# Input tokens stored as one contiguous piece per load, and the last output bank's last products done in two halves

## The reference

```python
hidden = relu(x @ wi.T + 2*(x @ common_wi_a.T) @ common_wi_b.T + 2*(x @ Ab.T) @ Bb.T)   # 256 -> 1024
h      = hidden @ wo.T + (the same two corrections)                                     # 1024 -> 256
probs  = softmax(h.mean(axis=1) @ gate_w);  top_w, top_i = top_k(probs, 2);  top_w /= top_w.sum()
y      = sum over the 2 chosen e of  top_w[e] * (gelu(h @ w1[e] + b1[e]) @ w2[e] + b2[e])
return x + y
```

## Time and profile before

| what | us |
|---|---|
| median of 3 runs (lowest, highest) | 267.82 (267.65, 268.33) |
| the profiled execution | 267.44 |
| its span in the trace, first to last event | 265.6 |
| what lies around the span | 1.8 |
| PE busy | 261.0 |
| DVE / ACT / POOL busy | 173.7 / 174.7 / 160.7 |

### The profile page before, as it was taken

The page is one execution under the profiler, slowest core; times in us unless marked ns, Lnnn a source line. Parts: engine busy times, 40 slices in busy tenths (PEclk is TensorE's granted clock), DMA queues, the critical chain, the costliest instruction groups (busy, mean ns, idle before and its releaser), DMA issues.

```text
span 265.6 us, 3607 instructions
## 1 busy us (share of the span) xinstructions
PE 261.0 (98%) x1150; PEld 212.7 (80%) x1150; DVE 173.7 (65%) x283; ACT 174.7 (66%) x279; POOL 160.7 (60%) x192
## 2 busy tenths in 40 slices
PE   8999999999999999999999999999999999999994
PEld 2778888888888888888888888888888888888883
DVE  0783767375999726667595866657856567565664
ACT  2757464555466379988986887676777677675650
POOL 2076998934389877798539999456366366331100
PEclk9999999999999999999999999999999999999999
DMA  5995120201042112201202112202202206000004
GB/s 185 346 389 202 42 79 0 84 1 39 0 123 79 12 67 82 79 16 64 83 0 50 65 46 79 79 0 82 69 13 79 79 2 199 0 0 2 0 1 158
DMA packets 11139, 19.76 MB, mean 74 GB/s; under 512 B 2000, under 2 KB 2256, under 8 KB 10992
## 3 DMA queue, kind: packets, MB, share of 16 engines
q1 hardware_dynamic: 10544, 18.61, 20.9%
q10 hardware_dynamic: 576, 0.92, 1.0%
HBM read 17.43 MB, written 2.10 MB: 74 GB/s over the span
## 4 chain that ended last, share of the span: by engine, by line
PE 98%; DVE 0%; DVEq 0%; issue 0%
PE out_ps L754 16%; PE out_ps L755 16%; PE out_ps L758 16%; PE hid_ps L754 14%; PE hid_ps L755 14%; PE hid_ps L758 14%; PE hid_ps L943 2%; PE hid_ps L794 1%; PE out_ps L872 1%; PE hid_ps L798 1%; PE hid_ps L802 1%; PE hid_ps L894 1%; PE hid_ps L884 1%; DVE x_sb L1242 0%; DVEq L130 0%; DVE y_sb L1143 0%
## 5 line engine op out<-in xcount | busy, mean ns | idle before, releaser
L409 POOL TENSOR_TENSOR up_lo<-up_raw,up_hi 128x512 fp32r<-128x512 f32 x41 | 52.9, 1312 | 37.5 <-ACT up_hi L569 37.4
L754 PE MATMUL out_ps<-hid_hi,down_hi 128*128 128x512 f32 x192 | 75.0, 390 | 0.0
L755 PE MATMUL out_ps<-hid_lo,down_hi 128*128 128x512 f32 x192 | 74.8, 390 | 0.0
L758 PE MATMUL out_ps<-hid_hi,down_lo 128*128 128x512 f32 x192 | 74.8, 390 | 0.0
L754 PE MATMUL hid_ps<-act_hi,up_hi 128*128 128x512 f32 x166 | 65.0, 392 | 0.0
L755 PE MATMUL hid_ps<-act_lo,up_hi 128*128 128x512 f32 x166 | 64.8, 390 | 0.0
L758 PE MATMUL hid_ps<-act_hi,up_lo 128*128 128x512 f32 x166 | 64.7, 390 | 0.0
L601 ACT ACTIVATE hid_ps<-hid_ps,bias_sb 128x512 f32<-128x512 f32 x64 | 42.2, 659 | 29.1 <-DVE hid_ps L1064 18.0
L1038 DVE SCALAR_TENSOR_TENSOR hid_lo<-hid_ps,mix,hid_hi 128x512 fp32r<-128x512 f32 x64 | 47.9, 748 | 20.2 <-ACT hid_hi L615 19.6
L415 POOL TENSOR_TENSOR down_lo<-down_raw,down_hi 128x512 fp32r<-128x512 f32 x24 | 32.3, 1348 | 37.2 <-ACT down_hi L579 37.2
L615 ACT ACTIVATE hid_hi<-hid_ps,mix 128x512 fp32r<-128x512 f32 x64 | 44.1, 689 | 4.7
(11 more groups left out here) (91 smaller groups left out, 237.0 us busy)
## 6 DMA issues: line engine op xcount, KB each, us to landing
up_raw<-in_w SPq DMA_DIRECT2D x16, 256.0 KB, 2.7
down_raw<-in_w SPq DMA_DIRECT2D x16, 256.0 KB, 2.5
lora_raw<-in_lora SPq DMA_DIRECT2D x10, 256.0 KB, 5.0
down_raw<-in_woT SPq DMA_DIRECT2D x8, 256.0 KB, 3.4
up_raw<-in_wiT SPq DMA_DIRECT2D x7, 256.0 KB, 4.3
outT<-x_sb SPq DMA_DIRECT2D x6, 256.0 KB, 3.6
x_sb<-in_xT SPq DMA_DIRECT2D x1, 1024.0 KB, 8.4
x_sb<-in_xT SPq DMA_DIRECT2D x1, 512.0 KB, 5.6
```

What stands on the lines that cost most here:

```text
L409: ins = eng.tensor_tensor(up_lo[:, n, cols], up_raw[:, n, cols], f32(up_hi[:, n, cols]), ALU.subtract)
L754: eng.matmul(out, w_h, a_h, start=start, stop=False, skip_group_check=onto)
L755: eng.matmul(out, w_h, a_l, start=False, stop=False, skip_group_check=onto)
L758: return eng.matmul(out, w_l, a_h, start=False, stop=stop, skip_group_check=onto)
```

## The change

The host stores `x` in three arrays instead of one: `x0T` [2 blocks, 128, 512] for the two loads of L262, `x0bT` [128, 2, 512] for the load of L327, and `x1T` for sequence 1. Each of the first three loads then reads one unbroken piece of DRAM. The load of sequence 1 was unbroken already. Number, order, size and queue of the DMAs stay.

At the end, the last output bank (1,1) is treated otherwise. Its sum in `out_ps[:, 3]` ends with set 22 (the `stop` mark moves there). A new function `last_half` makes the last set's products for this bank over 256 tokens at a time, the first half into bank 0 of `hid_ps` and the second into bank 1, whose hidden tiles have been read by then. Each half raises `s_done`. DVE first adds the bank of set 22, the bias and `x` over all 512 tokens (`with_bias`, semaphore `s_last`), right after its last `hid_low`, and later adds each half with a plain two-operand addition.

```diff
 def load_x0(eng, kd):
-    eng.dma_start(x_sb[:, 0, 0, kd, :], xT[0, :, 0, kd, :]).then_inc(s_x0[kd], 16)
+    eng.dma_start(x_sb[:, 0, 0, kd, :], x0T[kd, :, :]).then_inc(s_x0[kd], 16)
...
-            eng.dma_start(x_sb[:, 0, 1, :, :], xT[0, :, 1, :, :]).then_inc(s_x0b, 16)
+            eng.dma_start(x_sb[:, 0, 1, :, :], x0bT[:, :, :]).then_inc(s_x0b, 16)
...
+        LAST_BANK = {3: 0, 4: 1}
...
+                ends = q in GROUP_LAST or (q == NSET - 2 and (kd, t) == ENDS[-1])
                 return three(out_ps[:, bank, :], (down_hi[:, n, cols], down_lo[:, n, cols]),
                              (hid_hi[:, j, :], hid_lo[:, j, :]), q in GROUP_FIRST and j == mine[0],
-                             q in GROUP_LAST and j == mine[1], low_ready)
+                             ends and j == mine[1], low_ready)
+
+            def last_half(n):
+
+                q, (kd, _, toks) = NSET - 1, FINAL[n]
+                for j in (1, 3):
+                    f = tiles(q)[j][0]
+                    cols = slice(f * D + kd * P, f * D + (kd + 1) * P)
+                    ins = three(hid_ps[:, LAST_BANK[n], toks], (down_hi[:, q % ND, cols], down_lo[:, q % ND, cols]),
+                                (hid_hi[:, j, toks], hid_lo[:, j, toks]), j == 1, j == 3)
+                ins.then_inc(s_done, 1)
...
-                for kd in range(KD):
-                    for j in (1, 3):
-                        if kd == 0:
-                            eng.wait_ge(s_hid_lo, 4 * q + j + 1)
-                        ins = down_pair(q, j, kd)
-                    ins.then_inc(s_done, 1)
+                for j in (1, 3):
+                    eng.wait_ge(s_hid_lo, 4 * q + j + 1)
+                    ins = down_pair(q, j, 0)
+                ins.then_inc(s_done, 1)
+                for n in LAST_BANK:
+                    last_half(n)
...
+            def with_bias(kd, t, cols):
+                x = x_sb[:, NB - 1, t, kd, cols]
+                return eng.scalar_tensor_tensor(out=x, in0=out_ps[:, kd * NT + t, cols],
+                                                scalar=mixed_b2[:, NB - 1, 1, kd:kd + 1], in1=x,
+                                                op0=ALU.add, op1=ALU.add)
+
+
+            eng.wait_ge(s_down, 4 * (NSET - 1))
+            with_bias(*ENDS[-1], slice(0, TOK)).then_inc(s_last, 1)
             for n, (kd, t, cols) in enumerate(FINAL):
-                x = x_sb[:, NB - 1, t, kd, cols]
-                eng.wait_ge(s_done, ENDS.index((kd, t)) + 1)
-                eng.scalar_tensor_tensor(out=x, in0=out_ps[:, kd * NT + t, cols],
-                                         scalar=mixed_b2[:, NB - 1, 1, kd:kd + 1], in1=x,
-                                         op0=ALU.add, op1=ALU.add).then_inc(s_final, 1)
+                eng.wait_ge(s_done, n + 1)
+                if n not in LAST_BANK:
+                    with_bias(kd, t, cols).then_inc(s_final, 1)
+                else:
+                    x = x_sb[:, NB - 1, t, kd, cols]
+                    eng.wait_ge(s_last, 1)
+                    eng.tensor_tensor(x, hid_ps[:, LAST_BANK[n], cols], x, ALU.add).then_inc(s_final, 1)
...
+    by_partition = x.reshape(NB, S // TOK, TOK, D // P, P).transpose(0, 4, 1, 3, 2)
     arrays = {
         "ids": a["itok_B_0_7"].reshape(1, NB),
-        "xT": x.reshape(NB, S // TOK, TOK, D // P, P).transpose(0, 4, 1, 3, 2),
+        "x0T": by_partition[0, :, 0].swapaxes(0, 1),
+        "x0bT": by_partition[0, :, 1],
+        "x1T": by_partition[1],
```

More of the change, by code:

```diff
@@ L17, with build @@
 TOP_K = 2
-def build(nc, ids, xT, wiT, woT, early, lora, gate, w1, w2, b12, outT):
+def build(nc, ids, x0T, x0bT, x1T, wiT, woT, early, lora, gate, w1, w2, b12, outT):
     D, NTOK = outT.shape
@@ L198, in build @@
         s_x0hi, s_up0hi = sem("s_x0hi"), sem("s_up0hi")
-        s_r2, s_r3, s_add, s_hid_lo, s_merge, s_raw_lo, s_sum_lo, s_fin, s_final = (
-            sem(n) for n in ("s_r2", "s_r3", "s_add", "s_hid_lo", "s_merge", "s_raw_lo", "s_sum_lo", "s_fin", "s_final"))
+        s_r2, s_r3, s_add, s_hid_lo, s_merge, s_raw_lo, s_sum_lo, s_fin, s_final, s_last = (
+            sem(n) for n in ("s_r2", "s_r3", "s_add", "s_hid_lo", "s_merge", "s_raw_lo", "s_sum_lo", "s_fin", "s_final",
+                             "s_last"))
         s_up0lo, s_merge0, s_tok = sem("s_up0lo"), sem("s_merge0"), sem("s_tok")
@@ L336, in _ @@
             load_lora(0, 4, e)
-            eng.dma_start(x_sb[:, 1, :, :, :], xT[1, :, :, :, :])\
+            eng.dma_start(x_sb[:, 1, :, :, :], x1T[:, :, :, :])\
                .then_inc(s_x1, 16)
```

## The result

The changed kernel takes 266.70 us (median of 21, 265.86 to 267.52); the kernel before, timed beside it, 268.33 (median of 21, 266.85 to 271.15). The ratio is 0.9941, 95% interval 0.9923 to 0.9958: 1.6 us less, where 0.4 was forecast.

What follows compares the result with a forecast made beforehand. The prediction took PE's work plus the stretches before its first and behind its last instruction as the bound. Its terms, loads 0, DVE -0.36, extra addition 0, last store -0.05, gave -0.4 from 267.82: 267.4 us, range 266.9 to 268.2.

Steps and rivals of the forecast that it cites:

- The end: Last output bank, its additions and last store: DVE -0.36 us and store -0.05 us, together about -0.4 us.
- Pace of the halves: PE's last bank: twelve matmuls of 256 columns start 0.12 us apart, so PE ends 0.08 us later.
- DVE's last result: Behind PE's end only one addition of 0.44 us remains, so the last store can be issued 0.36 us earlier.
- The additions of 512: DVE's extra addition over 512 tokens fits into its gaps and does not move the third addition: 0 us.
- The last store: With the DMA engines nearly to itself it lands slightly sooner: 0 to -0.2 us, taken as -0.05.
- (a): Rival, last bank: halved matmuls pay the full weight load; chance 0.06 at 268.2 us or beyond, 0.05 at 267.7.
- (b): Rival, end: stores bunch and the last one's landing grows by what it was issued earlier; no gain, 267.8 us, chance 0.12.
- surplus of 390 ns: Last bank: by the skill's issue gaps, twelve halves would cost PE 390 ns more than six wholes, instead of 80.
- The loads of x: 0 us: Start of the kernel: faster loads of x gain nothing; bounds -0.3 and +0.1 us.
- the dummy matmuls hide all three: Start: dummy matmuls and PE's first products cover all three changed loads of x, so their landing does not matter.
- slack of 0.8 us: Third load of x: PE takes its operand 0.8 us after it is ready, so a load that much slower costs nothing.
- Rival (c): An earlier third load of x removes PE's pause at 18.45 us: another 0.3 us less, 267.1 us, chance 0.12.

Runs made afterwards that it cites:

- e2: The changed kernel with the loads of x as before, so only the last output bank in halves: 267.96 us, ratio 0.9997 to the kernel before.
- e1: The kernel before with only the loads of x made unbroken, its end unchanged: 266.86 us, ratio 0.9944.
- e14: The kernel before, unchanged, profiled again; one of its long executions: 270.93 us.
- e13: The kernel before with the load of lora_first moved behind the two strided loads of x on SP's queue: 273.86 us, ratio 1.0187.
- e7: The kernel before with lora_first, always of expert 0, loaded as ACT's first DMA, loads of x strided: 267.18 us, ratio 0.9955.
- e12: The kernel before, unchanged, profiled again: 268.16 us.
- e6: The kernel before with only the third load of x (512 KB, second token half) made unbroken: 268.89 us, ratio 1.0009.
- e3: The whole changed kernel timed once more, on the same chip as its parts: 266.54 us, ratio 0.9926 to the kernel before.
- e5: The kernel before with only the two 256 KB block loads of x made unbroken: 267.44 us, ratio 0.9953.
- e10: The kernel before with only the load of x of block 1 (SP's second DMA) made unbroken: 267.45 us, ratio 0.9975.
- e11: The changed kernel with 9 dummy matmuls instead of 12: 266.22 us, ratio 0.9914 to the kernel before.
- e16: The changed kernel with 10 dummy matmuls instead of 12: 266.46 us, ratio 0.9918 to the kernel before.
- e9: The kernel before with only the load of x of block 0 (ACT's first DMA) made unbroken: 267.49 us, ratio 0.9969.
- e8: The changed kernel with 24 dummy matmuls instead of 12: 269.03 us, ratio 1.0025 to the kernel before.

## Why the prediction was wrong

**The end: right, by its steps.** Pace of the halves 0.12: 0.119. DVE's last result 0.36 earlier against PE's first product of the last bank: 0.39, since the addition took 0.42 and not 0.44. The additions of 512 didn't move the third one: it starts 0.20 us behind the last bank's first matmul in both profiles. The last store: -0.05 was taken, 0 was seen. The sum of 0.4 was 0.4 in the profiles; the timings of e2 alone can't tell it from zero. Rivals (a) and (b) fell, and with the first the rule of the Trainium skill that was weighed there ("TensorE: Matmul & The Clock Gate", "Back-to-back issue gap"): in place of its surplus of 390 ns stand 12 x 0.119 - 6 x 0.226 us, 70 ns.

**The loads: the step that failed.** "The loads of x: 0 us" was -1.2 (1.6 less the end) to -1.5 (the ratio of e1). The bound for it was -0.3. The lower end of the range rests on that bound; the words behind it (267.1 less 0.3) give 266.8 and not the 266.9 that is written, and 266.7 lies below both. Three things in that step were wrong.

First, it asked who waits for x and not what else is delayed by moving x. The load of `lora_first` stands between those of x, and PE's first real product needs it. Its name was in the list of DMAs, its landing (2.65 + 2.8 = 5.5) against the dummies' end (6.4) was never set down as a cover of 0.9 us that could shrink. With the unbroken block loads `lora_first` took 2.0 to 2.2 us to its landing where it had taken 2.7 to 4.1, and landed by 5.2 where it had landed at up to 6.7. e14 and e13 show what a late landing costs, and with `lora_first` ahead of all, in e7, no execution had a mean granted clock under 0.998.

Second, "the dummy matmuls hide all three" took the dummies' end of one execution, 6.44, as a fixed time. It was among the latest of all profiles; it ranges from 5.3. In an execution where they end early, landings are waited for that would have been covered: in e12 that of the third load, 0.3 us later than in the profile of before with PE 0.6 earlier; in e6 that of the second, which was itself 2.6 us later. The slack of 0.8 us that was read for the third load was that of a profile with one of the longest covers. Rival (c) had named the third load, but through PE's pause at 18.45, at a price of 0.3; that pause is still there after the change. In e12, where PE waits behind the third load, the rest is 1.3 us longer. Its "against" (behind the first tiles everything is released by PE again) was wrong as well: DVE's factor work, once late, kept PE waiting at L894 and L754.

Third, the clock. No row of before showed a granted clock other than 1.0, and a pause of PE at the start was priced at its own length. In e14 a wait of 1.04 us was followed by 3 us of lost pace (rest 262.4 against 259.3 to 259.4). Of the 105 executions of before timed here, 28 have a mean granted clock of 0.994 or less, and their times are 268.9 to 271.3; of e1, e3 and e5, the kernels with both block loads unbroken and 12 dummies, none of 35. Setting these 28 aside, the mean of before falls from 268.5 to 268.1. So these executions, with their waits and the pace lost behind them, are about 0.4 us of the mean gain. That each of them had such a wait is inferred: of executions of that kind only e14, beside the 105, is profiled. The mean of e1 is 267.0, another 1.1 us below the 268.1 of the others; that is left for the earlier start and the waits for x.

What stays open: how the gain divides between the two block loads, and whether the third adds to it, how it divides between `lora_first` and the waits for x, why SP issued `lora_first` 0.3 us later (2.95 for 2.65) in most profiles with an unbroken first load and 1.3 us later in e10's, and whether the 269.8 and 270.1 us of e11 and e16, at a mean clock of 1.0, are waits of PE; no profile fell on them.

## What to carry to other kernels

A cover read from one profile is one draw: before a load is called hidden, set its landing beside the earliest end of what hides it, and do that for every load in flight beside it, the unchanged ones above all, because a faster transfer can pay where the next one lands. A spread of the timed executions that is wider than the profile explains (here 4 us, against 1.7 after) is itself a row to be read: ask which wait is there in some executions only. A pause ahead of the first real products is priced with the clock that may be lost behind it, not with its length.

## What the runs showed of the hardware

- A load of [128 partitions x 2 KB] took 3.4 to 3.5 us from issue to landing as the first DMA when its pieces of 2 KB lay 8 KB apart in DRAM, and 2.6 to 2.8 us when they lay one behind another. The size of the pieces is the same. The load issued 0.4 us behind it on the same queue, unchanged, took 3.6 to 3.8 us beside the first kind and 2.9 beside the second.
- One DMA's layout shows in its neighbours' landings: 96 KB issued between two strided loads landed after 2.7 to 4.1 us, with both block loads unbroken after 2.0 to 2.2 in every profile, and with only one of them unbroken after 2.3 (e9) and 2.1 (e10).
- Twelve dummy matmuls took 4.10 to 5.30 us in different executions; the starts of their weight loads are 0.43 us apart at first, and in the profile of the changed kernel four of them stand within 0.75 us from 4.06 us on, though the granted clock reads 1.0 throughout. 0.43 us is also what a matmul of 512 columns takes in e14 where the granted clock is 0.50 (0.85 for two). The trace's record of the clock begins only near the moment at which the dummies speed up (3.95 us there, 7.19 in e8), so that column doesn't show the lower level at the start of a kernel; the spacing does.
- PE's clock fell to its lower level (0.50 of 2.4 GHz) behind a pause of 1.04 us in e14 and within one of 3.55 us in e13, and not behind one of 1.13 us, between real products, in e6. The length of the pause alone doesn't tell.
- A matmul of 256 columns with its own 128 x 128 weights keeps a pace of 0.119 us over twelve in a row; one of 512 columns 0.226.
